# Two drains of TensorE taken out of the feed-forward block of a sandwich transformer layer on eight cores

## The reference

```python
x = x + _layernorm(attn(_layernorm(x), qkv_w, qkv_b, out_w, out_b))
x = x + _layernorm(ffn(_layernorm(x), gate_w, gate_scale, up_w, up_scale, down_w, down_scale))

def ffn(hidden_state, ...):
    Wg = (gate_w - 128) * gate_scale[:, None]     # (8192, 2048)
    Wu = (up_w - 128) * up_scale[:, None]         # (8192, 2048)
    Wd = (down_w - 128) * down_scale[:, None]     # (2048, 8192)
    g = einsum('bsh,ih->bsi', hidden_state, Wg)
    u = einsum('bsh,ih->bsi', hidden_state, Wu)
    h = silu(g) * u
    return einsum('bsi,hi->bsh', h, Wd)
```

## Time and profile before

| what | us |
|---|---|
| median of the two runs shown | 9252.99 |
| the two runs | 8885.46 and 9620.51 |
| the profiled execution | 8892.74 |
| its span, slowest core (core 4) | 8891.2 |
| spans of the eight cores | 8785.3 to 8891.2 |

### The profile page before, as it was taken

One profiled execution on the slowest core, in us unless ns is written; L12 is line 12 of the kernel. 1 busy time (PEld: TensorE's weight loads), 2 busy tenths in 40 slices (PEclk: granted clock), 3 DMA queues, 4 the chain that ended last, 5 costly groups with the idle time before them and its releaser, 6 DMA issues. The chain is left out here.

```text
span 8891.2 us, 82000 instructions; the slowest of 8 cores (8785.3 to 8891.2 us)
## 1 busy us (share of the span) xinstructions
PE 6711.0 (75%) x29698; PEld 2714.4 (31%) x30208; DVE 2625.1 (30%) x5232; ACT 1672.7 (19%) x2574; POOL 729.0 (8%) x1231
## 2 busy tenths in 40 slices
PE   0085565829777777777777586999799879988997
PEld 0032222314222322322322232333233323333333
DVE  4300000010566666666666341110211011101101
ACT  6310100101223233233223161000100010000001
POOL 0000000000000000000000000015001400240024
PEclk9998787969666666666666698999899989999998
DMA  7912522061100000000000345546554645464544
GB/s 221 213 48 62 102 55 57 29 123 45 51 16 16 25 18 16 16 28 16 16 28 4 136 154 134 122 107 148 134 131 100 155 117 133 101 163 121 122 104 134
DMA packets 686308, 781.93 MB, mean 88 GB/s; under 512 B 235062, under 2 KB 636534, under 8 KB 659128
## 3 DMA queue, kind: packets, MB, share of 16 engines
q0 software_dynamic: 421216, 470.06, 21.6%
q1 hardware_dynamic: 264696, 306.59, 12.8%
HBM read 407.41 MB, written 117.44 MB: 59 GB/s over the span
## 5 line engine op out<-in xcount | busy, mean ns | idle before, releaser
L932 PE MATMUL d_pgu<-d_ha,d_wd 128*128 128x512 bf16 x4012 | 916.0, 388 | 26.2 <-DMA d_wd<-down_u 20.1
L893 PE MATMUL d_pgu<-d_l,d_wg 128*128 128x512 bf16 x3984 | 920.3, 381 | 10.3 <-issue 6.6
L904 PE MATMUL d_pgu<-d_l,d_wu 128*128 128x512 bf16 x4024 | 924.8, 380 | 3.8
L420 PE MATMUL b_pspt<-b_id,b_pb 128*128 128x128 bf16 x5120 | 606.7, 281 | 210.7 <-DVE b_ptb L526 200.9
L1022 DVE TENSOR_SCALAR d_ua<-d_pgu,d_su 128x512 bf16<-128x512 f32 x256 | 192.3, 751 | 1786.5 <-PE d_pgu L904 1786.5
L234 PE MATMUL A2K_pa<-A2K_X,A2K_W 128*128 128x512 bf16 x1004 | 226.3, 384 | 571.9 <-DMA A2K_X<-ln1x_s 570.9
L234 PE MATMUL A2V_pa<-A2V_X,A2V_W 128*128 128x512 bf16 x2000 | 463.9, 392 | 241.6 <-DMA A2V_X<-ln1x_s 238.7
L832 POOL DMA_DIRECT2D d_wd<-down_u x1024 | 542.8, 571 | 753.5 <-PE d_pgu L932 731.9
L526 DVE COPY b_ptb<-b_pspt 128x512 bf16<-128x512 bf16 x1280 | 527.1, 423 | 226.2 <-PE b_pspt L420 219.8
L932 PEld LDWEIGHTS d_pgu<-d_ha,d_wd 128*128 128x128 bf16 x4096 | 405.1, 100 | 539.6 <-issue 95.9
L420 PEld LDWEIGHTS b_pspt<-b_id,b_pb 128*128 128x128 bf16 x5120 | 425.2, 121 | 415.6 <-issue 369.9
(11 more groups left out here) (160 smaller groups left out, 6195.1 us busy)
## 6 DMA issues: line engine op xcount, KB each, us to landing
d_wg<-gate_u POOLq DMA_DIRECT2D x64, 2048.0 KB, 9.7
d_wu<-up_u POOLq DMA_DIRECT2D x64, 2048.0 KB, 14.5
d_wd<-down_u POOLq DMA_DIRECT2D x1024, 128.0 KB, 2.4
a_xt<-x_seq SPq DMA_DIRECT2D x32, 1024.0 KB, 7.1
ln1x_s<-a_lnx SPq DMA_DIRECT2D x32, 512.0 KB, 7.7
a_xt<-x_own SPq DMA_DIRECT2D x16, 1024.0 KB, 7.1
A2K_Wf<-qkv_w POOLq DMA_DIRECT2D x16, 1024.0 KB, 11.3
k_s<-A2K_st SPq DMA_DIRECT2D x32, 512.0 KB, 2.6
```

What stands on the lines that cost most here:

```text
L420: ins = t.transpose(pspt[:, (tg % 2) * 1024 + r_ * 128: (tg % 2) * 1024 + (r_ + 1) * 128], PB[:, pb0 + r_ * S + tk * 128: pb0 + r_ * S + ( ...
L893: ins = t.matmul(psG, WG[:, (sxg % 2) * 8192 + hh * 512 + i * 128: (sxg % 2) * 8192 + hh * 512 + (i + 1) * 128], L3T[:, hh * 512:(hh + 1) ...
L904: ins = t.matmul(psU, WU[:, (sxg % 2) * 8192 + hh * 512 + i * 128: (sxg % 2) * 8192 + hh * 512 + (i + 1) * 128], L3T[:, hh * 512:(hh + 1) ...
L932: ins = t.matmul(psD[:, hm * 512:(hm + 1) * 512], WD[:, ((idg % 2) * 8 + ii) * 512 + hm * 128: ((idg % 2) * 8 + ii) * 512 + (hm + 1) * 128 ...
```

## The change

It takes two drains out of TensorE's list, the one ahead of the first and the one ahead of the second column sum of each pass. With four passes these are eight instructions per core. The waits ahead of them stay. Nothing is added, and nothing else moves: TensorE's other instructions, and those of the other engines, stand in the same order with the same waits.

```diff
@@ -868,7 +868,6 @@
                 t.wait_ge(l3l, 256 * (tc + 1))
                 if tc >= 1:
                     t.wait_ge(dv, 16 * tc)
-                t.drain()
                 for hh in range(16):
                     ins = t.matmul(psD[0:1, 0:512], ONC[:, :],
                                    L3T[:, hh * 512:(hh + 1) * 512],
```

## The result

The changed kernel took 9195.2 us (median of 11 runs, 9027.8 to 9733.09) beside 9079.91 us (10 runs, 8885.46 to 9620.51) for the kernel before. The ratio is 1.0272, with a 95% interval from 1.0182 to 1.0362. It leaves out executions in which one die is over 1% behind the other, or that are over 1.5% above the fastest of their kernel. So the change came out slower, clear of no change, where none was forecast; whether by over 2%, the interval leaves open. The same comparison was made again later, on chip 0, with a copy of the changed kernel and gave 1.0004 (0.9972 to 1.0035). The rest of this document is about how both can be.

A forecast was written before the change was run, and what follows sets the result against it. The prediction took TensorE's matmuls to bound the feed-forward block, with time to win only in gaps. From the profiled 8892.74 us it subtracted 8 x 0.07 = 0.56 us, giving 8892.2 us; own range 8870 to 8905, measured range 8868 to 9635 us.

The forecast's parts named there:

- A drain costs 0.07 us here, 0.56 us in all: Ahead of both column sums: each of eight drains costs 0.07 us of issue, so removal wins 0.56 us.
- The 0.08 us of the records: Lower reading for the eight drains at both column sums: their recorded durations, 13 and 8 ns, sum to 0.08 us.
- The scatter of the hand-over, and the lower bound of -0.7 us: Issue ahead of line 923 varies, 0.14 to 0.25 us; least kind comparisons at both drains give a 0.7 us loss.
- First rival, 4.075 us each: Both drains cost what line 940's does, 4.075 us each, 32.6 us in all, giving 8860.1 us; chance 0.02.
- What is late next: Ahead of the column sums, input and `d_ha` still come last; the waits of 202.0 and 6.5 us stay.
- 8892.2 us, own range 8870 to 8905 us: Whole kernel: likeliest time 8892.2 us, chance 0.74; own range covers the hand-over bounds and clock cases.
- the wide range: Whole kernel's measured time: 8868 to 9635 us, set by how the program repeats between its two runs.
- Within 2% with 0.95, slower with 0.03: Whole kernel: chance 0.95 of within 2%, 0.03 of slower and 0.02 of faster by over 2%.
- The clock as a rival: TensorE's clock behind second column sums and after input waits gets better, 8874.5 us (0.08), or worse, 8898.1 us (0.10).
- The second and third rival: Second: three clock falls (3.3 us each) and three late rises (2.6 us each) avoided, 0.08; third: the reverse, 0.10.
- Its sign of being wrong altogether: Feed-forward block: a new TensorE wait, or its length changing by more than 20 us on most cores.
- the third rival: Second pass loses its clock behind the second column sum, fourth pass's rise comes late: 5.9 us slower, 8898.1 us; chance 0.10.

The follow-up runs named there:

- the copy's profile: Profile of the changed kernel run again, differing from it only in a comment; 8875.84 to 9691.65 us, median 9338.91 us of 7 runs.
- zeros in the block: The kernel before with only the gate, up and down weights set to zero; 8880.67 to 9081.6 us, 7 runs.
- the last copy of the changed kernel: The changed kernel for a third time, on chip 0 and real data; 8849.94 to 9730.25 us, 16 runs, ratio 1.0004 to before.
- the copy of before: The kernel before run again, differing only in a comment; 8887.63 to 9422.9 us, median 9307.14 us of 6 runs.
- its later copy: The kernel before copied again for the third comparison, on chip 0, no instruction changed; 8872.0 to 9594.9 us, 7 runs.
- 33 drains: The kernel before with 33 drains in place of one at each of the two places; 8897.56 to 9659.4 us, median 9322.77 us of 6 runs.

## Why the prediction was right or wrong

- **A drain costs 0.07 us here, 0.56 us in all.** Right for one drain; the 0.56 us in all is eight times that, and no run can see it in the kernel's time. The gaps shrank by 0.07 us at both places, and 32 further drains cost 0.072 us each. The 0.08 us of the records would have been wrong by seven times, and the Trainium skill's rule (Perfetto Trace Analysis, section Sequencer-only Instruction (DRAIN, etc)), that a record holds only the execution, chose the right view.
- **The scatter of the hand-over, and the lower bound of -0.7 us.** Misread. What the prediction took for scatter is the number of waits. At the start of the down products line 923 has one wait ahead of it in the first pass (line 918) and two in the later ones (line 921 too). In the first group of gate and up line 888 has two in the first pass (lines 877 and 880) and four in the later ones (lines 886 and 887 too), where the prediction counted two. The chain of the first pass, before:

```profile
5406.32 0.21 issue
5406.52 6.51 PE d_pgu L873 x16
...
5414.62 0.25 issue
5414.87 0.37 PE d_pgu L888
```

  | ahead of | waits | drain | issue, us |
  |---|---|---|---|
  | L923, first pass | 1 | no | 0.14 |
  | L888 first pass; L923 second pass | 2 | no | 0.25 |
  | L888 third pass | 4 | no | 0.46 |
  | L914; L873 first pass | 1 | yes | 0.21 |
  | L873 third pass | 2 | yes | 0.32 |

  A further wait costs 0.11 us and the drain 0.07 us in all of these rows; the same places in all four passes and on all eight cores differ from them by 0.03 us at most. Compared at equal waits, the trace of before gave 0.07 us at both places, and no row stood behind a loss.
- **First rival, 4.075 us each.** Wrong by a factor of 57, as its own row suggested. That the 4.075 us are the time of the matmuls still under way shows in the changed kernel: on core 0 the same drain (now line 938) has up to 4.928 us, and the clock there is 0.81.
- **What is late next.** Right: the waits for the input and for `d_ha` end the gaps as before.
- **8892.2 us, own range 8870 to 8905 us.** Right only for an execution that stays free of long stretches at 0.81. The profiled copies of the changed kernel took 8875.84 us, with none, and 8849.94 us, which is 20 us under the own range and has 146 us at 0.81 on each of two cores. So eight cores repeat less well than that range allows. The median of 9195.2 us lies in the wide range, which was as wide as the program's two executions; that is no success of the sum. Cores with a mean clock of 0.822 and more span 8848.2 +- 2.2 us before (286 cores) and 8853.3 +- 2.8 us changed (131 cores).
- **Within 2% with 0.95, slower with 0.03.** Here the prediction failed. The step is the sum itself: 8892.74 - 0.56 starts from an execution near the lower of two and has no term for what sets the other 735 us higher. That went into the width of the range as mere repetition, without a cause, and 2% was taken as what a measurement can tell. What stood there is a level of the clock, 0.81, worth 186 us a core in the changed kernel's profile. Before had four executions near 8890 us among ten, the changed kernel none among its first. Three of its executions had both dies held down alike, by 170 to 280 us (9057.79, 9167.74 and 9169.21 us); their mean over the mean of those four is 1.027. The 2.7% is the price of a partly disturbed execution, and not of the drains.
- **The clock as a rival.** The right resource, the wrong level and place. The second and third rival moved the clock between 1.00 and 0.55 at the second column sum, for 3.3 us a time. What came was a third level, 0.81, over stretches of up to hundreds of us, in any stage with matmuls.
- **Its sign of being wrong altogether.** The block's length was to change by no more than 20 us on most cores. In the changed kernel's profile it grew by over 100 us on six of eight, though the account of the drains is right; in the copy's profile, without the level of 0.81, it changed by under 23 us on every core. A sign read from times says nothing before the clock is held equal.
- Did those small falls change? A fall was counted where the clock records have 0.50 between the end of the second sum and the 50th down matmul. Of the profiles on real data, five with the second drain have 126 in 160 passes, four without have 106 in 128: 79% and 83%. With zeros in the block it is 89 in 128 and 26 in 32, and in all 75% and 82%, a difference of twice its error. That leans to the third rival; if it is real it is 0.08 x 4 x 3.3 = 1.1 us per core, more than the drains' removal wins, and the spans above can neither show nor exclude that. It stays open.

## What to carry to other kernels

Before a difference is explained, compare the mean granted clock of each core, and whether the difference already stands in stages ahead of the change. If the spread between executions is many times what a change can move, a copy of the unchanged kernel, and a run on zeros, are the first experiments and not the last. Compare hand-overs only at equal numbers of waits: here each further one takes 0.11 us. A drain behind a wait for work that depended on the same engine has nothing to drain and costs only its own hand-over: here 0.07 us.

## What the hardware showed that was not expected

**A third level of TensorE's clock.** Beside 1.00 and 0.50 the trace has 0.81 (0.8125), on real data and never on zeros: none in the profiles of four runs on zeros, 32 cores in all, and no core with a mean clock under 0.822 in the 30 executions. The Trainium skill has it: TensorE: Matmul & The Clock Gate, section Seeing it yourself, tells of a limiter that takes a whole die to 13/16 of its clock once three of its cores run dense matmuls, and says that zeroed operands don't trip it. The traces agree in the level and in the zeros. They don't always agree in the whole die: the last copy of the changed kernel has it in one stretch of 160 us (146 of them at 0.81), on cores 0 and 1, and none on cores 2 and 3 or on the other die. I didn't weigh that rule in the prediction, and the two executions 735 us apart were what called for it.

**It looks like the overlap of two pairs of cores.** Cores 0 and 1 show the level in nearly the same stretches of their own time (within some tens of us) in every profile that has it, and so do 2 and 3, 4 and 5, 6 and 7; the two pairs of a die show it at different times. In the changed kernel's profile cores 4 and 5 have it from 476 to 1710 us, cores 6 and 7 from 7770 to 9000 us. Shift one by 7294 us and the two fall on each other, and 9047 us, the end of core 7, then stands at 1753 us of core 4's time. The pattern on cores 0 and 2 fits with a shift of 2835 us. Two windows of the same length, 2835 us apart, on core 0 and on core 2:

```profile
8300.00:8490.00 190.00, 190.00 (x694) 67.12 (x693) 22.35 (x38) 13.74 (x20) 9.13 (x8) 0.81 0.47 110
```
```profile
5465.00:5655.00 190.00, 188.44 (x680) 67.11 (x693) 23.54 (x40) 13.05 (x19) 10.44 (x10) 0.81 0.45 103
```

In three more disturbed profiles a die's pairs fit likewise: with shifts of 6291 and 3547 us in the copy of before, 5772 us in its later copy, 2644 and 2238 us with 33 drains. The match is not exact. In six of these seven the beginnings agree within 10 us and in one they lie 54 us apart; three ends agree within 11 us, the other four lie 64 to 137 us apart. The reading is that the pairs of a die start apart, and that the clock falls while the tail of one runs beside the head of the other; whether a run is disturbed is then decided by how far apart they started. That is worked out from where the stretches lie, as each core's trace has a time of its own. No run set the distance, so it isn't shown, and two things speak against it as it stands: the 160 us on one pair alone, named above, and that nearly equal shifts bring unequal amounts (with 2835 us 1343 to 1486 us at 0.81, with 2644 us 2320 to 3034).

**What that level costs.** From no disturbance (8850 to 8930 us) up to 9718.01 us for before and 9733.09 us for the changed kernel, some 9%. The mean clock of a core gives its span: a line through all 560 core spans of before has 8826 us at 0.83, 9096 us at 0.80 and 9546 us at 0.75; through the 288 of the changed kernel 8827, 9104 and 9566 us.
